# Column sums of v in the statistics stage: three of seven tiles summed on TensorE, four on VectorE

## The reference, cut to what matters

```python
def _bn(x, gamma, beta):
    mu = jnp.mean(x, axis=0)
    var = jnp.mean(jnp.square(x - mu), axis=0)
    return gamma * (x - mu) * jax.lax.rsqrt(var + EPS) + beta
z = jnp.concatenate([node_feats[src], node_feats[dst], edge_feats], axis=1)
gate = jax.nn.sigmoid(_bn(z @ W_int + b_int, g_int, be_int))
upd = jax.nn.softplus(_bn(z @ W_upd + b_upd, g_upd, be_upd))
```

## Time and profile before

| | us |
|---|---|
| median of 3 runs | 12580.16 |
| lowest and highest run | 12571.6, 12588.71 |
| the profiled execution | 12564.72 |
| its span, from first to last instruction | 12563.0 |
| the 288 steps of the statistics, first and last sum of v (line 1360) | 3474.8 to 4621.9 |

### The profile page before, as it was taken

How to read it: one execution, slowest core, us unless ns; L and a number is a source line. 1 busy time by engine, 2 the same in 40 slices (tenths; PEclk the granted TensorE clock), 3 DMA queues, 4 the chain that set the end, 5 groups by cost and what they waited for, 6 DMA issues and landing times. The chain is left out here.

```text
span 12563.0 us, 438885 instructions
## 1 busy us (share of the span) xinstructions
PE 7912.2 (63%) x149095; PEld 7405.0 (59%) x149106; DVE 8207.7 (65%) x17786; ACT 6913.4 (55%) x17614; POOL 5175.5 (41%) x4482
## 2 busy tenths in 40 slices
PE   6444444488855549995766656666666666565765
PEld 6333333488745448885656656565665566565765
DVE  6777777588799999981750762925718527358047
ACT  1222222299855559986217448965479764587530
POOL 2777777444300001110630752706707338345044
PEclk8555555599978879998979669787697787787997
DMA  5555543299967759987949999979999799997997
GB/s 205 166 171 167 169 140 84 83 348 348 326 195 202 201 173 319 323 275 264 346 127 349 288 262 354 297 263 300 284 324 316 226 329 290 290 335 231 366 361 226
DMA packets 1430365, 3241.49 MB, mean 258 GB/s; under 512 B 392074, under 2 KB 973252, under 8 KB 1419042
## 3 DMA queue, kind: packets, MB, share of 16 engines
q1 hardware_dynamic: 1054798, 2289.98, 52.1%
q0 software_dynamic: 331264, 823.09, 24.7%
q10 hardware_dynamic: 44116, 125.96, 3.3%
HBM read 2042.53 MB, written 1129.76 MB: 253 GB/s over the span
## 5 line engine op out<-in xcount | busy, mean ns | idle before, releaser
L1956 POOL DMA_INDIRECT mask_cols<-cols_all,mask_index x864 | 1372.1, 1588 | 1339.1 <-ACT mask_index L1965 1172.0
L521 POOL DMA_INDIRECT rows_s<-place_rec,place_index x1568 | 1631.1, 1040 | 538.1 <-issue 528.7
L596 PE MATMUL place_slot_ps<-place_runs,place_oh_turned 50*128 50x100 f32 x3136 | 725.8, 423 | 1231.6 <-DVE place_runs L635 1213.6
L2104 POOL DMA_INDIRECT hop_x<-cols_all,hop_index x864 | 981.2, 1136 | 1237.4 <-ACT hop_index L2111 920.0
L596 PEld LDWEIGHTS place_slot_ps<-place_runs,place_oh_turned 50*128 50x128 f32 x3136 | 683.0, 327 | 1265.9 <-issue 1265.6
L2120 ACT ACTIVATE hop_parts<-hop_x,mask 128x64 f32<-128x64 f32 x5184 | 1265.4, 334 | 47.6 <-DMA hop_x<-cols_all,hop_index 28.1
L2047 DVE SCALAR_TENSOR_TENSOR mask_hidden<-mask_cols,att 128x448 f32<-128x448 f32 x864 | 538.5, 623 | 1085.5 <-DMA mask_cols<-cols_all,mask_index 1028.8
L2167 PE MATMUL hop_sums_ps<-hop_parts,hop_onehot 128*128 128x64 bf16 x18144 | 876.0, 216 | 472.3 <-DVE hop_parts L2149 398.2
L2167 PEld LDWEIGHTS hop_sums_ps<-hop_parts,hop_onehot 128*128 128x128 bf16 x18144 | 777.0, 113 | 573.6 <-issue 572.7
L1478 POOL DMA_DIRECT2D cm_onehot<-hot_d x288 | 152.1, 528 | 2031.1 <-POOLq L104 1229.9
L2014 PE MATMUL mask_part_ps<-mask_now,mask_turned 128*128 128x64 bf16 x18144 | 912.5, 231 | 37.4 <-issue 20.9
(11 more groups left out here) (392 smaller groups left out, 26453.3 us busy)
## 6 DMA issues: line engine op xcount, KB each, us to landing
cols_all<-att_in_rows SPq DMA_DIRECT2D x216, 896.0 KB
mask_onehot<-hot_s SPq DMA_DIRECT2D x216, 896.0 KB
cols_all<-hop_in_rows SPq DMA_DIRECT2D x216, 896.0 KB
hop_onehot<-hot_s SPq DMA_DIRECT2D x864, 224.0 KB
rows_all<-blank SPq DMA_DIRECT2D x72, 1808.0 KB
ct_u<-rows_all SPq DMA_DIRECT2D x288, 452.0 KB
cm_v<-rows_all SPq DMA_DIRECT2D x288, 448.0 KB
cm_onehot<-hot_d POOLq DMA_DIRECT2D x288, 448.0 KB
```

The lines of the kernel that those rows point to most:

```text
L521: nc.gpsimd.indirect_dma_start(m.rows_s.rearrange("p n w -> (p n) w"), bass.IndirectOffsetOnAxis(index[:, j, t:t + 1], 0), rec[:, j, t, :] ...
L596: last = nc.tensor.matmul(slot_ps[b][:, t, 0:2 * NBK], oh_turned[:, b, t, :], runs[:, b, t, :], start=True, stop=True)
L1956: nc.gpsimd.indirect_dma_start(cols[:, n, :], None, table, bass.IndirectOffsetOnAxis(index[:, n, :], 0), compute_op=ALU.add).then_inc(arri ...
L2104: nc.gpsimd.indirect_dma_start(x[:, n, :, :].rearrange("p c f -> p (c f)"), None, table, bass.IndirectOffsetOnAxis(index[:, n:n + 1], 0)). ...
```

## The change

The sum of v is divided. VectorE goes on summing tiles 0 to 3 of each batch (`OWN = 4`, 512 elements of 896). Tiles 4 to 6 (384 columns) are fed to TensorE as the moving operand of one float32 matmul with the float32 identity as the weights, and it adds them up in a PSUM bank of its own over all 288 steps. TensorE does this for batch `it - 1` right after the spread of batch `it`. VectorE waits for it before it overwrites that v buffer two steps later. A matmul with zeros opens the bank at the start and another closes it at the end, and VectorE copies the 384 sums to the last three tiles of `sum_acc`.

```diff
+        totaled = sem("totaled")
+        OWN = 4
+        total_ps = ctx.enter_context(nc.psum_tensor("ct_total_ps", [P, 512], fp32))[:, 0:(BATCH - OWN) * W].rearrange("p (c w) -> p c w", w=W)
...
             @block.vector
             def _(dve):
                 dve.sem_inc(valued, 2)
+                dve.sem_inc(totaled, 2)
...
                     dve.wait_ge(spread, it + 1)
                     dve.wait_ge(squared, it + 1)
+                    dve.wait_ge(totaled, it + 1)
                     dve.sem_inc(gate, 1)
                     nc.vector.tensor_tensor(v[:, i % 2, :, :], v_ps[i % 2][:], u[:, i, 0:C * W].rearrange("p (c w) -> p c w", w=W),
                                             ALU.add).then_inc(valued, 1)
...
-                    nc.vector.tensor_tensor(sum_acc[:], sum_acc[:], v[:, i % 2, :, :], ALU.add).then_inc(summed, 1)
+                    nc.vector.tensor_tensor(sum_acc[:, 0:OWN, :], sum_acc[:, 0:OWN, :], v[:, i % 2, 0:OWN, :], ALU.add).then_inc(summed, 1)
...
                 add_squares(IT - 1, 1)
+                dve.wait_ge(totaled, IT + 3)
+                nc.vector.tensor_copy(sum_acc[:, OWN:BATCH, :], total_ps)
...
             @block.tensor
                     last.then_inc(spread, 1)
+                    if not isinstance(it, int) or it > 0:
+                        add_up(it - 1, (i - 1) % 2)
+
+                def add_up(it, j):
+                    pe.wait_ge(valued, it + 3)
+                    pe.sem_inc(gate, 1)
+                    nc.tensor.matmul(total_ps.rearrange("p c w -> p (c w)"), m.ident[:], v[:, j, OWN:BATCH, :].rearrange("p c w -> p (c w)"),
+                                     start=False, stop=False).then_inc(totaled, 1)
+                add_zeros(nc, m, total_ps, True)
                 turn_in(0, 0)
-                each4(pe, step)
+                each4(pe, step, first=1)
+                add_up(IT - 1, (IT - 1) % 2)
+                add_zeros(nc, m, total_ps, False).then_inc(totaled, 1)
```

## The result

| | before | after |
|---|---|---|
| median of 6 runs, us | 12584.26 | 12534.05 |
| lowest and highest | 12571.6, 12589.0 | 12514.64, 12538.14 |
| the profiled execution (span) | 12564.72 (12563.0) | 12514.64 (12513.0) |

The change makes the kernel 50 us faster: the ratio is 0.9959 with a 95% interval of 0.9946 to 0.9972. The forecast was 12520 with 59 us of gain.

A forecast was written before the change was run, and what follows sets the result against it. VectorE's four passes were taken to bound the statistics stage; with the load loop next, steps go from 3.997 to 3.79 us, 287 steps gain 59 us, and 12580.2 - 59 = 12521, rounded 12520; range 12458 to 12585.

The forecast's parts named there:

- VectorE as the bound of before: In the statistics stage, VectorE's four passes set the step of the kernel before, 3.997 us.
- 0.40 us less of VectorE's work: VectorE's sum goes from 1.00 to about 0.60 us, its work a step from 4.00 to 3.60.
- The load loop: v, square, load of u, one-hots, v two steps on: 7.56 us for two steps, giving back about half the gain.
- The signs: What the profile after would show in the stage: sum 0.73 us, VectorE idle some 50 us, busy about 95%.
- the load term: In the load loop, the load of u takes 3.90 us from issue to one-hots, read at the stage's start.
- v to issue: In the load loop, the next load of u is issued 2.66 us after v starts.
- its own narrow range: The forecast proper for the stage: 3.74 to 3.86 us a step, 12505 to 12540 us, chance 0.60.
- the second rival: The load of u takes nearly its 4.36 us: nothing gained, 12580; at 4.1 us, 12546; chance 0.13 with middle ground.
- The load by the Trainium skill: Load of u estimated at 3.06 us, so it lands in time and the sum's whole 115 us is gained.
- TensorE's matmul in idle time: The added float32 matmul, 0.72 us plus 0.2 to 0.3 for weights, lies in TensorE's idle time and costs nothing.
- The new wait, ScalarE, start and end at nothing: VectorE's wait for TensorE's sum, ScalarE's turned copy, opening matmul and final copy in the stage: zero cost.
- The third rival: TensorE at half clock in the stage needs 4.75 us a step: slower, 12616, up to 12650; chance 0.10.

The follow-up runs named there:

- E5: The kernel before, with the load of u issued after the copy of the map column instead of after the square: 12590.39 us, ratio 1.0005.
- E1: The changed kernel, with the load of u issued after ScalarE's copy of the map column instead of after its square: 12440.1 us, ratio 0.991.
- E3: The changed kernel, with the load of u issued later, behind ScalarE's copy of the node block: 12534.29 us, ratio 0.9986.
- E2: The kernel before, with VectorE's sum cut to tiles 0 to 3 and tiles 4 to 6 summed by nobody: 12478.58 us, ratio 0.9944.
- E6: The changed kernel, with VectorE summing all seven tiles beside TensorE's sum of three: 12582.35 us, ratio 1.0003 to the kernel before.
- E4: The changed kernel again without an edit, on another chip than E5 to E8: 12485.17 us, ratio 0.9941 to the kernel before.
- E7: The changed kernel with the early load of E1, VectorE summing two tiles and TensorE five: 12430.24 us, ratio 0.9878 to the kernel before.
- E8: The changed kernel with the early load of E1, TensorE summing all seven tiles and VectorE none: 12424.28 us, ratio 0.9877 to the kernel before.

## Why the prediction was right

- **VectorE as the bound of before.** Right: E5, where a shorter load loop changed nothing.
- **0.40 us less of VectorE's work.** Right: the one-hots start 0.60 us after the sum's start where nobody waits, and E1 runs at 3.598 us.
- **The load loop is late next and takes back about half.** Right: 3.819 us measured, 3.79 forecast. The waits stand before line 1343, released by the load of u. E1 and E3 move the load alone by -0.86 and +0.40 us and the step follows, down to VectorE's own work in the one and by half of the delay in the other.
- **The signs.** The forecast had 0.73 us for the sum, some 50 us idle, 95% busy and 0.4 us for each record of the matmul; the changed kernel shows 0.68, 44, 94.4 and 0.52.
- **The size of the load term.** Too small: I took 3.90 us from the stage's start, and over all loads it is 4.12 to the start of the one-hots. The term v to issue was too large, 2.66 against 2.53. Together 2.53 + 4.12 + 1.00 = 7.65 us for two steps, 3.82, where I had 7.56, or 7.58 with the 0.01 a step for scatter. This sum proves nothing by itself: the three terms fill two steps in any kernel of this order, and in E5, where nobody waits, they are 1.89 + 5.11 + 1.00. That the load sets the step is shown by the waits and by E1 and E3. But the packets show the load's own time: in the changed kernel its last one ended 3.56 us after the issue in the mean, and in the late steps the one-hots started 0.52 us (median) behind the last packet, so the load took some 4.1 us.
- **Luck in the sum.** With a load of 4.1 us the prediction itself has 3.88 us a step and 12546, outside its own narrow range, under the second rival. The step stayed at 3.82 because v to issue fell by 0.12 us, from 2.65 in the kernel before. That was not foreseen. ScalarE's copy starts 0.23 us after the recorded end of v in both kernels, and v's mean recorded length fell from 1.20 to 1.08 us when VectorE was no longer full. So two errors, 0.22 and 0.13 us, partly cancelled, and 9 us between the 59 forecast and the 50 measured are left.
- **The load by the Trainium skill.** The estimate of 3.06 us from the Trainium skill's page DMA: Bandwidth & Descriptors (section Anatomy of one DMA — SWDGE (gpsimd) path) would have made the load hidden. The trace does not agree: 4.27 us in the step shown, for which VectorE waited.
- **TensorE's matmul in idle time.** Right: 0.86 us for both records (0.72 plus an open weight load forecast), and E2 and E6 price it at nothing.
- **The new wait, ScalarE, start and end at nothing.** Right as far as the rows show: in front of v VectorE waits 3.3 us, once, as before, and from the last sum to the first matmul of line 1020 it is 3.0 us in both kernels (4621.9 to 4624.9, 4566.2 to 4569.2).
- **The third rival (TensorE at half clock).** It did not happen. The kernel before spends 434 us of this stage at the lower level, E5 419 and E2 246, none of them with the matmul. With it, E1, E4, E6, E7 and E8 have no such stretch after the stage's start, the changed kernel one of 3.4 us and E3 seven. In the one of the changed kernel (first the window, then TensorE and VectorE) the matmul took 1.59 us, as the prediction's 1.31 + 0.3 had it:

```profile
4243.90:4247.30 3.40, 3.40 (x26) 2.56 (x24) 3.40 (x5) 2.25 (x4) 0.00 (x0) 0.51 0.70 195
4243.69 2.20 PE L1421 MATMUL ct_v_ps<-ct_now,ct_turned 128*128 128x128 bf16 x21
4245.68 1.59 PE L1430 MATMUL ct_total_ps<-ct_v,ident 128*128 128x384 f32 x2
4246.75 1.08 DVE L1359 TENSOR_TENSOR ct_v<-ct_v_ps,ct_u 128x896 f32<-128x896 f32 x1
```

VectorE did not wait for a product there. What longer stretches at half clock would cost with the matmul no run shows.

## What to carry to other kernels

Shortening the full engine's work pays only down to the next loop through its buffers. Before the edit, add up that loop (last reader of a buffer, issue, landing, first use, and so on) and divide by the number of steps it spans. If it lies between the new and the old step, search at the same time for a reader that releases the buffer too late: here one semaphore on the right instruction was worth 45 us on top of 72 on the same chip, and it was worth nothing before the change. Where no wait shows how long a load takes, bound its time from both sides, and expect it to differ from one chip to another. And when the terms of a loop always add up to its steps, the sum is no proof: move one term and see whether the step follows.

## What had not been expected

- The mean recorded length of VectorE's passes over 896 elements was 1202 ns in the kernel before, 1082 in the changed one and up to 1302 in the median of E5, while the start-to-start distance of a full engine was 1.00 us in all three. The recorded length of one instruction on a full engine isn't its cost. But for those who wait for it it counts: in all ten kernels traced, ScalarE's copy started 0.23 us in the mean after the recorded end of v, so a longer v also delays the square and the next load.
- The load of 452 KB took 3.56 us from its issue to the end of its last packet in one place and 3.39 in another, in the same kernel, and 4.12 and 3.96 us to its use.
- In the kernel before, the granted clock fell to 0.50 again and again, 50 times in the stage, after stretches at 1.00 in which TensorE had work in every step and was 45% busy. With one more matmul a step (E6, 61% busy) it was 1.00 in the windows of the stage looked at.
